# Cross-attention and a mixture of experts: one feature of the normalised rows becomes a constant that carries b1, and all experts run in fp16 halves

## The reference, cut to what matters

```python
def layernorm(x): m = mean(x); v = var(x); return (x - m) / sqrt(v + 1e-5)

# B, L, D = 8, 256, 128 declared; x and ctx are (32, 64, 128)
def xattn(ctx, x, Wq):
    q = x @ Wq.T; k = v = ctx @ Wq.T
    scores = where(causal, q @ k.T / sqrt(128), -inf)
    return softmax(scores) @ v

def ffn(x, gate_W, W1, b1, W2, b2):            # 8 experts, W1[e] 128x256, W2[e] 256x128
    gates = softmax(x @ gate_W)
    cw = the two largest gates of a row, divided by their sum; 0 elsewhere
    out = x
    for e in range(8):
        out = out + cw[:, e:e+1] * (relu(x @ W1[e] + b1[e]) @ W2[e] + b2[e])
    return out

x = x + xattn(ctx_1024, layernorm(x), Wq)
x = x + ffn(layernorm(x), gate_W, W1, b1, W2, b2)
```

## Time and profile before

| | us |
|---|---|
| median of 3 runs | 132.61 |
| lowest and highest | 131.99, 133.05 |
| the profiled execution | 132.61 |
| its span (first to last instruction) | 130.8 |
| TensorE busy | 122.1 (93%) |
| VectorE busy | 106.1 (81%) |
| ScalarE busy | 93.2 (71%) |
| GpSimd busy | 53.1 (41%) |

### The profile page before, as it was taken

One profiled execution on the slowest core, in us unless ns is written; L12 is line 12 of the kernel. 1 busy time (PEld: TensorE's weight loads), 2 busy tenths in 40 slices (PEclk: granted clock), 3 DMA queues, 4 the chain that ended last, 5 costly groups with the idle time before them and its releaser, 6 DMA issues. The chain is left out here.

```text
span 130.8 us, 3269 instructions
## 1 busy us (share of the span) xinstructions
PE 122.1 (93%) x1165; PEld 92.1 (70%) x1165; DVE 106.1 (81%) x415; ACT 93.2 (71%) x189; POOL 53.1 (41%) x57
## 2 busy tenths in 40 slices
PE   6987798999989999999999999999999979999991
PEld 2674576777857769778877868778766757777690
DVE  0619998989999996968898996958998799867683
ACT  3247466999576955797679954994799558989830
POOL 7198156320084950321095840330277503345400
PEclk9999999999999999999999999999999999999999
DMA  3999900000000000200000000200000003000002
GB/s 95 319 286 295 291 28 8 0 0 0 5 0 0 0 8 0 80 0 5 0 0 5 0 3 0 80 5 0 0 3 8 0 0 85 3 0 0 5 0 80
DMA packets 9904, 5.54 MB, mean 42 GB/s; under 512 B 504, under 2 KB 9888, under 8 KB 9888
## 3 DMA queue, kind: packets, MB, share of 16 engines
q1 hardware_dynamic: 9744, 5.27, 14.7%
q10 hardware_dynamic: 144, 0.07, 0.2%
HBM read 4.28 MB, written 1.05 MB: 41 GB/s over the span
## 5 line engine op out<-in xcount | busy, mean ns | idle before, releaser
L658 POOL TENSOR_TENSOR h_lo<-h,h_hi 128x512 f16<-128x512 f32 x24 | 28.7, 1195 | 41.7 <-ACT h L543 41.3
L543 ACT ACTIVATE h<-psH,b1T 128x512 f32<-128x512 f32 x64 | 43.4, 690 | 1.1 <-PE psH L482 0.9
L542 ACT ACTIVATE h_hi<-psH,b1T 128x512 f16<-128x512 f32 x48 | 33.1, 689 | 14.9 <-PE psH L361 14.9
L832 DVE SCALAR_TENSOR_TENSOR acc<-psY,weight_y,acc 128x128 f32<-128x128 f32 x125 | 35.1, 341 | 3.2 <-PE psY L382 3.1
L357 PE MATMUL psH<-x_hi,w_hi 128*128 128x512 f16 x62 | 23.5, 379 | 1.0 <-ACT h L543 1.0
L816 DVE TENSOR_TENSOR h_lo<-h,h_hi 128x512 f16<-128x512 f32 x24 | 16.5, 688 | 8.8 <-ACT h L543 8.5
L361 PE MATMUL psH<-x_lo,w_hi 128*128 128x512 f16 x62 | 23.5, 379 | 0.0
L358 PE MATMUL psH<-x_hi,w_lo 128*128 128x512 f16 x62 | 23.5, 379 | 0.0
L382 PE MATMUL psY<-w_hi,h_hi 128*128 128x128 f16 x192 | 22.7, 219 | 0.0
L382 PE MATMUL psY<-w_lo,h_hi 128*128 128x128 f16 x192 | 22.7, 219 | 0.0
L382 PEld LDWEIGHTS psY<-w_hi,h_hi 128*128 128x128 f16 x192 | 15.4, 98 | 2.2
(11 more groups left out here) (175 smaller groups left out, 187.6 us busy)
## 6 DMA issues: line engine op xcount, KB each, us to landing
w_sb<-in_L_ffn_W_dram SPq DMA_DIRECT2D x8, 256.0 KB, 4.9
out_dram<-acc SPq DMA_DIRECT2D x3, 256.0 KB, 2.3
x_sb<-in_x_dram SPq DMA_DIRECT2D x2, 256.0 KB, 4.5
ctx_sb<-in_ctx_dram SPq DMA_DIRECT2D x2, 256.0 KB, 4.8
x_sb<-in_x_dram SPq DMA_DIRECT2D x1, 512.0 KB, 6.8
ctx_sb<-in_ctx_dram SPq DMA_DIRECT2D x1, 512.0 KB, 7.5
out_dram<-acc SPq DMA_DIRECT2D x2, 128.0 KB, 1.8
wq_sb<-in_L_xattn_Wq_dram ACTq DMA_DIRECT2D x1, 64.0 KB, 2.9
```

The source lines that it names most:

```text
L542: nc.scalar.activation(h_hi[:, C * (e % 2) + c, :], psH[c][:, :], ACT.Relu, bias=bias, scale=scale)
L543: nc.scalar.activation(h[:, C * (e % 2) + c, :], psH[c][:, :], ACT.Relu, bias=bias, scale=scale).then_inc(h_ready, 1)
L658: nc.gpsimd.tensor_tensor(h_lo[:, i, :], h[:, i, :], h_hi[:, i, :], ALU.subtract).then_inc(hlo0_ready, 1)
L832: last = nc.vector.scalar_tensor_tensor(out=o, in0=y, scalar=weight_y[:, g % 2, t, e:e + 1], in1=o, op0=ALU.mult, op1=ALU.add)
```

## The change

A row of normalised features sums to zero, so feature 127 is minus the sum of the others, and x @ W1 = sum over the first 127 of x_i (W1[i] - W1[127]). The change uses that. Row 127 of the tile `w1_sb` now holds b1, `x_hi` holds the constant `SX` in its partition 127 (`x_lo` zero), and the other 127 rows of W1 and of the gate have row 127 subtracted. For this W1 is loaded as 127 rows, and row 127 is loaded once more, repeated into 127 partitions (`w1_last`). GpSimd subtracts (`w1_centred`). ScalarE's Relu then needs no bias and `b1T` goes. All experts are split. The low half of a chunk is made by VectorE straight from `psH` where `LO_DVE` says so (chunk 1 of e=1, 4 and 6, and both chunks of the last expert), and ScalarE then skips its second reading; elsewhere by GpSimd from `h`. Some steps move on VectorE, ScalarE and GpSimd at the start, and some slots by one to three.

```diff
-    SX, SW, SH = 16.0, 64.0, 16.0
-    FULL = (0, 3)
-    FULL_LAST = (0, 7)
+    SX, SW1 = 2.0, 8.0
+    SH, SW2 = SX * SW1, 64.0
+    SC, SB = 16.0, 64.0
+    LO_DVE = (0, 1, 0, 0, 1, 0, 1, 0)
...
+    def lo_on_dve(n, c):
+        if n == GROUPS * E - 1:
+            return True
+        return c == 1 and LO_DVE[n % E] > 0
...
             def weights(p):
                 e = slice(2 * p, 2 * p + 2)
-                sp.dma_start(w1_sb[:, e, :], w1_v[:, e, :]).then_inc(w1_in[p], 16)
+                sp.dma_start(w1_sb[0:D - 1, e, :], w1_v[0:D - 1, e, :]).then_inc(w1_in[p], 16)
+                sp.dma_start(w1_last[0:D - 1, e, :],
+                             w1_v[D - 1:D, e, :].broadcast_to([D - 1, 2, HID])).then_inc(w1_in[p], 16)
+                sp.dma_start(w1_sb[D - 1:D, e, :], b1[e, :].unsqueeze(0)).then_inc(w1_in[p], 16)
...
                 for c in range(C):
-                    pe.wait_ge(h_ready, u + c - 1)
+                    if n and lo_on_dve(n - 1, c):
+                        pe.wait_ge(hlo_dve_ready, lo_count(True, n - 1, c))
+                    elif n:
+                        pe.wait_ge(h_ready, (n - 1) * C + c + 1)
...
-                        nc.scalar.activation(h_hi[:, C * (e % 2) + c, :], psH[c][:, :], ACT.Relu, bias=bias, scale=scale)
-                    nc.scalar.activation(h[:, C * (e % 2) + c, :], psH[c][:, :], ACT.Relu, bias=bias,
-                                         scale=scale).then_inc(h_ready, 1)
+                    i = C * (e % 2) + c
+                    hi = nc.scalar.activation(h_hi[:, i, :], psH[c][:, :], ACT.Relu)
+                    if lo_on_dve(n, c):
+                        hi.then_inc(h_ready, 1)
+                    else:
+                        nc.scalar.activation(h[:, i, :], psH[c][:, :], ACT.Relu).then_inc(h_ready, 1)
...
+            def w1_centred(p):
+                pool.wait_ge(w1_in[p], 16 * 3)
+                w = (slice(0, D - 1), slice(2 * p, 2 * p + 2), slice(None))
+                nc.gpsimd.tensor_tensor(w1_sb[w], w1_sb[w], w1_last[w], ALU.subtract).then_inc(w1c_ready, 1)
...
             first_rstd(0)
-            weights_hi(0)
-            weights_hi(1)
+            w1_centred(0)
+            w1_hi_part(0)
+            w2_hi_part(0)
+            w1_centred(1)
             for ts, banks in HALVES:
                 attention_rstd(0, ts)
             first_rstd(1)
             base_sum(0)
-            hidden_lo0(0, 0)
+            w1_centred(2)
+            hidden_lo(0, 0)
+            w1_centred(3)
...
+                        nc.vector.scalar_tensor_tensor(out=h_lo[:, i, :], in0=psH[c][:, :], scalar=0.0, in1=h_hi[:, i, :],
+                                                       op0=ALU.max, op1=ALU.subtract).then_inc(hlo_dve_ready, 1)
...
+            nc.vector.memset(x_hi[P - 32:P, :, :], SX).then_inc(ones_ready, 1)
+            nc.vector.memset(x_lo[P - 32:P, :, :], 0.0).then_inc(ones_ready, 1)
...
             for ts, banks in HALVES:
                 first_values(ts, banks)
                 mask_and_max(0, ts, banks)
-            w1_lo_part(0)
+            dve.wait_ge(x_in[1], 16)
+            for t in range(TG, 2 * TG):
+                last = row_stats(t)
+            chain.mark(last)
             small_parts()
```

More of the change, by code:

```diff
@@ L60, in xattn_moe, with lo_count @@
     w2_v = w2.rearrange("e (c p) n -> p (e c) n", p=P)
[L62 to L67, removed]
+    def lo_on_dve(n, c):
+        if n == GROUPS * E - 1:
+            return True
+        return c == 1 and LO_DVE[n % E] > 0
+    def lo_count(on_dve, n, c):
+        done = [(i, k) for i in range(n + 1) for k in range(C) if i < n or k <= c]
+        return sum(lo_on_dve(i, k) == on_dve for i, k in done)
     stack = ExitStack()
@@ L84, in xattn_moe @@
         gate_sb = sb("gate_sb", [P, E])
-        b1_rows = sb("b1_rows", [E * C, P])
         b2_rows = sb("b2_rows", [NB2, D])
         w1_sb = sb("w1_sb", [P, E, HID])
+        w1_last = sb("w1_last", [P, E, HID])
+        gate_last = sb("gate_last", [P, E])
         w2_sb = sb("w2_sb", [P, E, C, D])
@@ L367, in output_product @@
                 i = e % 2
[L368 to L372, removed]
+                pe.wait_ge(w2lo_ready, e // 2 + 1)
                 pe.wait_ge(h_ready, (n + 1) * C)
@@ L387, in output_product @@
                 for t in range(TG):
[L388 to L397, removed]
+                    add_product(t, h_hi, w2_hi, last_expert or t == 0, False)
+                    add_product(t, h_hi, w2_lo, False, False)
+                pe.wait_ge(hlo_pool_ready, lo_count(False, n, C - 1))
+                pe.wait_ge(hlo_dve_ready, lo_count(True, n, C - 1))
+                for t in range(TG):
+                    add_product(t, h_lo, w2_hi, False, last_expert or t == TG - 1)
             def probs_step(a):
@@ L519, in x_hi_part @@
                 cols = slice(ts[0] * P, (ts[-1] + 1) * P)
-                nc.scalar.activation(x_hi[:, a, cols], banks["xfT"][:, cols], ACT.Copy,
+                act.wait_ge(ones_ready, 2)
+                nc.scalar.activation(x_hi[0:D - 1, a, cols], banks["xfT"][0:D - 1, cols], ACT.Copy,
                                      scale=SX).then_inc(xhi_ready, len(ts))
@@ L556, in after @@
                 run(steps, g * SLOTS + slot)
+                if g == 0 and slot == W_HI[2]:
+                    w1_hi_part(2)
                 if g == 0 and slot == W_HI[3]:
@@ L651, in base_sum, with hidden_lo @@
                                         ALU.add).then_inc(base_ready, 1)
-            def hidden_lo0(g, e):
-                if is_split(g, e):
-                    i = C * (e % 2)
-                    pool.wait_ge(h_ready, (g * E + e) * C + 1)
-                    nc.gpsimd.tensor_tensor(h_lo[:, i, :], h[:, i, :], h_hi[:, i, :],
-                                            ALU.subtract).then_inc(hlo0_ready, 1)
+            def hidden_lo(g, e):
+                n = g * E + e
+                for c in range(C):
+                    if not lo_on_dve(n, c):
+                        i = C * (e % 2) + c
+                        pool.wait_ge(h_ready, n * C + c + 1)
+                        nc.gpsimd.tensor_tensor(h_lo[:, i, :], h[:, i, :], h_hi[:, i, :],
+                                                ALU.subtract).then_inc(hlo_pool_ready, 1)
             steps = [(FIRST_RSTD, 2, first_rstd), (RSTD, 1, lambda a: attention_rstd(a, ALL)), (BASE, 1, base_sum)]
@@ L757, in x_lo_part @@
                 cols = slice(ts[0] * P, (ts[-1] + 1) * P)
-                nc.vector.scalar_tensor_tensor(out=x_lo[:, a, cols], in0=banks["xfT"][:, cols], scalar=SX,
-                                               in1=x_hi[:, a, cols], op0=ALU.mult,
+                if a == 0:
+                    dve.wait_ge(ones_ready, 2)
+                nc.vector.scalar_tensor_tensor(out=x_lo[0:D - 1, a, cols], in0=banks["xfT"][0:D - 1, cols], scalar=SX,
+                                               in1=x_hi[0:D - 1, a, cols], op0=ALU.mult,
                                                op1=ALU.subtract).then_inc(xlo_ready, len(ts))
@@ L944, in _ @@
                 second_variance(0, ts, chain)
-            dve.wait_ge(x_in[1], 16)
-            for t in range(TG, 2 * TG):
-                last = row_stats(t)
-            chain.mark(last)
+            w1_lo_part(0)
             for ts, banks in HALVES:
                 second_norm(0, ts)
-            chain.wait()
             mean_and_var(TG, 2 * TG, chain)
```

92 lines of the change are left out of this document (44 added, 48 removed).

## The result

The changed kernel took 213.89 us (median of four, 213.54 to 214.25), the kernel before beside it 132.76 (four, 131.99 to 133.05). The ratio is 1.614, 95% interval 1.608 to 1.621. The forecast was 211.1, range 192 to 233.

What follows compares the result with a forecast made beforehand. TensorE was taken to bound the expert loop. Span 130.8 + 78.2 (late loads) + 2.0 (clock) - 2.6 (experts leaving fp32) + 0.9 (GpSimd low halves) = 209.3, and 1.8 more gave 211.1 us, range 192 to 233.

Steps and rivals of the forecast that it cites:

- The dealing of the loads: Start: each 127-row W1 or w1_last load goes to one DMA engine, 11.9 us each; chance 0.82, 211 us.
- eight engines side by side: Rival for the start: each 127-row load has one engine, another each time, so loads overlap; 138 us, chance 0.05.
- the ragged dealing: Start: 127 rows dealt over 16 engines unequally, 8 rows each and 7 on one; 0.74 us a load.
- Who waits: Start: VectorE and GpSimd stand behind late loads, delaying expert 1's low products from 28.35 to 106.6, +78.2 us.
- The 1.5 us of the start that I called covered: Start: extra wait for expert 0's low halves, hidden by load waits but +1.5 us if loads are dealt over all engines.
- unequal shares (132.4): Rival for the start: 127 rows dealt over all engines, +1.5 at the start, -2.6 + 0.9 in the loop; chance 0.08.
- TensorE after the pause: TensorE's restart: about four microseconds of work at half clock rate, +2.0 us, between 0 and 4.
- The loop: Expert loop after the restart: six experts leaving fp32 save TensorE 0.44 us each, -2.6; GpSimd's low halves cost +0.9.
- +0.9: Loop, around e=4: TensorE waits for GpSimd's low half, 0.3 us for each of three groups, range 0 to 2.5.
- the 0 for psH1: Loop, e=1, 4 and 6: VectorE's reading releases psH1 at about the old time, costing 0.
- My sign of being wrong: Loop: the term is wrong if TensorE waits for GpSimd's low halves in most experts.
- ScalarE, hidden at +1.4: ScalarE: evacuations go from 112 to 114 at 690 ns, +1.4 us at most, hidden on an engine busy 71%.

Runs made afterwards that it cites:

- e1_even_loads: The changed kernel with W1's 127 rows loaded as 112 and 15 rows and w1_last loaded into 128 partitions: 149.57 us, ratio 1.128.
- e4_gate_slots_back: e1_even_loads with the steps GATE_EXP, GATE_TOP, CHOICE and WEIGHTS back in their old slots: 149.62 us, ratio 1.128.
- e5_lo_on_gpsimd: e1_even_loads with GpSimd making both low halves of every expert but the last, LO_DVE all zeros: 150.59 us, ratio 1.135.
- e8_lo_as_before: e1_even_loads with low halves of chunk 0 on GpSimd, chunk 1 on VectorE from SBUF, psH freed by ScalarE; last expert unchanged: 150.87 us, ratio 1.132.
- e7_before_all_halves: The kernel before with no expert in fp32 (FULL and FULL_LAST empty), nothing else: 146.10 us, ratio 1.102.
- e9_two_experts_in_fp32: e1_even_loads with group 0 expert 1's chunk-1 low half moved to GpSimd and the earlier fp32 experts (0, 3; last group 0, 7) restored: 139.42 us, ratio 1.049.
- e10_before_only_3_in_fp32: The kernel before with only expert 3 in fp32 in groups 0 to 2, last group as it was: 133.48 us, ratio 1.003.
- e11_before_only_0_in_fp32: The kernel before with only expert 0 in fp32 in groups 0 to 2, last group as it was: 142.12 us.
- e12_fp32_and_lo_as_before: e9_two_experts_in_fp32 with low halves of chunk 0 on GpSimd and chunk 1 on VectorE from SBUF, as before: 138.86 us, ratio 1.046.
- e2_last_in_128: The changed kernel with only w1_last loaded into 128 partitions, W1 still in one load of 127 rows: 171.71 us.
- e3_before_in_127: The kernel before with W1 loaded as 127 rows and one row, nothing else: 157.24 us.

## Why the prediction was right

**The dealing of the loads (0.82, 211 us)** was right in mechanism. Counting completions against rows predicted that 127 rows go to one engine, and the counts, the rate and three edits of the shape agree. The rival "eight engines side by side" falls with it: the two loads of a pair come one after the other. By my own count alone the ragged dealing stayed possible, since the kernel before had no such load. The rate was low: I took 21.9 GB/s, the trace shows 23 to 26. From the reading of pair 1 to that of pair 3 it took 46.5 us, where my landings have 48.9. The landings I gave as 31, 55, 79.5 and 103.9; group 1's statistics start at 28.73, pair 1 to 3 are read at 52.26, 75.35 and 98.73. The restart is at 101.16 and not 106.6: **-5.4 us**.

**Who waits** was right item by item: GpSimd's w1_centred is what every stage stands behind. The subtraction, which I took at 1.5, is 1.26. The 1.5 us of the start that I called covered are covered here; without the cover (e1_even_loads and its kin) the start and the moved work cost more than that, not less: the low products of expert 1 begin at 38.02 there, 9.7 later than in the earlier trace rows. By its own time the rival "unequal shares (132.4)" was therefore wrong too: with its loads dealt out the kernel takes 149.6, not 132.4.

**TensorE after the pause (+2.0)** was right in kind: the products after the restart start 0.43 apart until about 106.7, 5.5 us at half rate, which is 2.8 lost; the granted clock of 100 to 108 us is 0.58, and 1.00 after it.

**The loop (-2.6, +0.9 and the 0 for psH1)** is the step that failed. I priced an expert that leaves fp32 at TensorE's own 0.44 us and thereby took it for the loop's only bound. The loop after the restart takes 110.7 us where the sum implied 102.7: **+8.0**, of which the clock is 0.8. What TensorE waits for in the changed kernel, from 106 us to the end, is

```profile
PE psH L370 <- DVE h_lo L836: 4.7, 5, 1.3
PE psD L348 <- DVE weight_cat L825: 3.0, 3, 1.1
PE psB L293 <- DVE xf L768: 0.4, 2, 0.2
```

and in the kernel before, from 30 us on:

```profile
PE psY L382 <- POOL h_lo L658: 0.7, 1, 0.7
PE psH L357 <- ACT h L543: 0.7, 1, 0.7
PE psD L344 <- ACT weight_catT L494: 0.2, 1, 0.2
```

So I had charged the wrong engine. After the restart TensorE never waits for GpSimd's low halves, for which the +0.9 stood. The release of psH1 by VectorE, which I put at 0, is 4.7 us, and the gate weights (weight_cat), which I did not price, are 3.0. The waits of a matmul grew by 6.5 us where I had 0.9; with the clock that names 6.4 of the 8.0, and 1.6 stay open. My sign of being wrong, TensorE waiting for GpSimd's low halves in most experts, did not come, and the term was wrong all the same.

These waits are where the loss shows, and not its cause: e4_gate_slots_back, e5_lo_on_gpsimd and e8_lo_as_before took single ones away, and the time stayed. That giving up the fp32 experts is a large part is measured in both kernels, -3.5 by my rows and +13.3 in e7_before_all_halves, 7.7 back in e9_two_experts_in_fp32. The chain behind it could be read in the kernel before: at the place of the earlier trace rows VectorE gets expert 3's low half ahead of the second variance, and expert 4's low half on GpSimd stands behind that. e10_before_only_3_in_fp32 and e11_before_only_0_in_fp32 show that expert 3 in fp32 is the cover for it. In the changed kernel GpSimd makes both halves of expert 3 and TensorE does not wait for it there, so this chain does not carry over as it stands; what makes VectorE late in that loop was not taken apart.

The two errors, -5.4 and +8.0, largely cancelled, which is luck: the time was closer than its terms. Either one alone would still have left the sum (219.1 or 205.7) within the range.

**ScalarE, hidden at +1.4** was hidden, but went the other way: 114 evacuations at 600 ns and not 690, 68.4 us against 76.5.

**The 6.0 us left open.** With even loads, fp32 experts and low halves as before, what still differs is b1's constant and the memsets, the subtraction of the last row, the extra traffic, and the moved slots. In the profiled execution of e12_fp32_and_lo_as_before the low products of expert 1 begin at 31.92, 3.6 later than in the earlier trace rows, and the loop from there is 3.2 longer. The gate's chain of group 0 on VectorE ends at 31.04 there and at 27.44 before, the same 3.6. It is late in two places. The first is the loads: VectorE waits for group 1's x, now read earlier, and for b2's rows,

```profile
11.67 0.87 DVE L724 BATCH_NORM_STATS2 stats<-x_sb 128x6 f32<-128x128 f32 x4 [1.00 <-DMA x_sb<-in_x_dram]
13.29 0.19 DVE L953 TENSOR_TENSOR gate_sb<-gate_sb,gate_last 128x8 f32<-128x8 f32 x1 [0.75 <-DMA b_rows<-in_L_ffn_b_dram]
```

and its first inv_sum starts at 15.17 where before it was 13.53, 1.6 later. The second is one w_lo operation, a low half of the weights, which takes 1.1 us longer, a mechanism that I did not price. VectorE's timeline in e1_even_loads has it,

```profile
23.53 1.79 DVE L929 SCALAR_TENSOR_TENSOR w_lo<-w_sb,w_hi 128x512 f16<-128x512 f32 x1
```

against GpSimd's:

```profile
23.51 1.26 POOL L681 TENSOR_TENSOR w_sb<-w_sb,w_last 127x512 f32<-127x512 f32 x1
```

The w_lo takes 0.69 us elsewhere (at 35.10 in this kernel). Here it begins 20 ns after a GpSimd subtraction and takes that one's 1.26 us longer, less 0.16. The page "SBUF — State Buffer" of the Trainium skill, section "SBUF: two separate sides", says that the two engines share a pair of ports under an exclusive lock, and that a VectorE operation with two SBUF inputs blocks fully while a GpSimd operation that reads SBUF holds it; this row agrees (0.69 + 1.1 = 1.79). The same operation takes 1.79 us in e12_fp32_and_lo_as_before too (at 23.78). So 1.6 and 1.1 of the 3.6 at the start can be read from the trace; no run undoes them, and the 3.2 in the loop stay open.

## What to carry to other kernels

Count what a DMA's leading dimension divides by before taking one row off it: 128 to 127 rows cost 5.5 to 10.6 us a load of 260 KB here (22.1 us for the four that e2_last_in_128 keeps, 24.7 for the four of e3_before_in_127, 42.2 for the four of w1_last in the changed kernel, which come on top of W1's), and 112 + 15 rows went back to sixteen and fifteen engines. When an operation is made cheaper on the bound engine, ask which engine's queue gets its by-products, and what is queued behind them; the slow form may be the cover of a chain on other engines. And when TensorE waits for a neighbour, moving the named operation may only rename the wait, where that neighbour is late with the next thing as well: here one such move gained 2.5 us, and the others nothing beyond the noise.

## What was unexpected of the hardware

- ScalarE's evacuation of a 128x512 bank takes 600 ns without a bias tile where it took 690 with one, for fp16 and fp32 output alike, and with a scale other than one too (600 for h of the fp32 experts in e9_two_experts_in_fp32).
- One engine alone moved 23 to 26 GB/s in most slices, more than a sixteenth of the best half-microsecond of all sixteen (21.9).
- A contiguous row of 2 KB (b1) left one completion; a row of two separate pieces of 1 KB left two.
- xf's normalisation (128x128 on VectorE) has a mean of 732 ns where it was 499 before; GpSimd makes 50 low halves beside it now, and 24 before. With 62 of them it is 974 ns (e5_lo_on_gpsimd), with 24 again 574 (e12_fp32_and_lo_as_before), but with 32 in e7_before_all_halves it is 509 and with 37 in e9_two_experts_in_fp32 739: it matters where they stand, and not only how many there are.
